# New step, piece and tile tables in the written order of an attention and FFN kernel

## The reference

```python
x = x + attention(layernorm(x))          # 16 heads of 16 features, causal
x = x + ffn(layernorm(x))
# attention: num = exp(rot(q) . rot(k) / 4), den = sum over ALL k of exp(q . k / 4), no rotation
#            y = where(causal, num / den, 0) @ v;   then y @ Wout + bout
# ffn: square(relu(x @ Ws1)) @ Ws2, and eight routed experts whose weight
#      trunc(softmax(top 2 logits)) is 0 except where one of the two weights is 1
```

## Time and profile before

| | us |
|---|---|
| median of 3 runs | 1680.91 |
| the profiled execution | 1680.97 |
| its span, first to last instruction | 1679.4 |
| ACT busy | 1586.1 (94%) |
| PE busy | 1487.9 (89%) |
| DVE busy | 848.6 (51%) |
| POOL busy | 526.9 (31%) |
| mean granted PE clock | 0.978 |

### The profile page before, as it was taken

One profiled execution on the slowest core, in us unless ns is written; L12 is line 12 of the kernel. 1 busy time (PEld: TensorE's weight loads), 2 busy tenths in 40 slices (PEclk: granted clock), 3 DMA queues, 4 the chain that ended last, 5 costly groups with the idle time before them and its releaser, 6 DMA issues.

```text
span 1679.4 us, 25467 instructions
## 1 busy us (share of the span) xinstructions
PE 1487.9 (89%) x8224; PEld 574.9 (34%) x8224; DVE 848.6 (51%) x1946; ACT 1586.1 (94%) x2639; POOL 526.9 (31%) x865
## 2 busy tenths in 40 slices
PE   2888989999999989999899999999999998999885
PEld 1322323333333333333343333333333333333323
DVE  5433434665346653566456553466535664455315
ACT  1899999999999999999999999999999999999990
POOL 3323233332233322333332322343223433333210
PEclk8998999999999999999999999999999999999997
DMA  5332332332434313333233234333143432332300
GB/s 160 97 120 91 94 114 91 124 94 76 129 104 138 111 38 123 122 121 104 89 116 123 95 91 130 114 116 104 51 129 114 129 114 65 115 123 82 95 26 26
DMA packets 95005, 172.05 MB, mean 102 GB/s; under 512 B 15504, under 2 KB 82064, under 8 KB 82576
## 3 DMA queue, kind: packets, MB, share of 16 engines
q1 hardware_dynamic: 94272, 169.15, 32.6%
q10 hardware_dynamic: 592, 1.18, 0.3%
HBM read 111.55 MB, written 58.72 MB: 101 GB/s over the span
## 4 chain that ended last, share of the span: by engine, by line
ACT 86%; PE 7%; issue 4%; DVE 2%; DMA 1%; SPq 0%; DVEq 0%; POOL 0%; ACTq 0%
ACT scores L488 56%; ACT probs L498 27%; ACT probs L500 3%; PE scores L544 2%; PE y_ps L573 1%; PE side L583 1%; PE scores L551 1%; PE side L602 0%; SPq L322 0%; DMA x_in<-in_L_attn_x 0%; PE scores L652 0%; DMA qk_parts<-parts 0%; PE scores L592 0%; PE scores L602 0%; DVEq L789 0%
## 5 line engine op out<-in xcount | busy, mean ns | idle before, releaser
L488 ACT ACTIVATE scores<-scores 128x1024 f32<-128x1024 f32 x1024 | 1067.1, 1119 | 24.5 <-PE scores L544 24.2
L544 PE MATMUL scores<-stack 96*128 96x512 bf16 x2048 | 584.6, 385 | 84.9 <-ACT scores L488 38.3
L498 ACT ACTIVATE probs<-scores 128x1024 f32<-128x1024 f32 x512 | 491.3, 1106 | 7.1 <-PE scores L551 5.7
L551 PE MATMUL scores<-stack 96*128 96x512 bf16 (+3 forms) x1536 | 337.3, 331 | 50.9 <-ACT scores L488 38.9
L394 POOL TENSOR_SCALAR_AFFINE_SELECT probs<-probs 128x256 f32<-128x256 f32 (+1 forms) x640 | 243.4, 408 | 392.4 <-ACT probs L498 224.5
L573 PE MATMUL y_ps<-probs,v_sb 128*32 128x512 f32 (+3 forms) x3072 | 331.8, 504 | 4.1 <-POOL probs L394 4.1
L544 PEld LDWEIGHTS scores<-stack 96*128 96x128 bf16 x2048 | 152.8, 97 | 493.8 <-ACT scores L488 203.5
L488 ACT ACTIVATION_READ_ACCUMULATOR scores<-scores 128x1 f32 x1024 | 297.3, 290 | 0.0
L404 POOL TENSOR_TENSOR parts<-rest,parts 128x512 bf16<-128x512 f32 x124 | 143.2, 1155 | 292.1 <-DVE parts L856 292.1
L551 PEld LDWEIGHTS scores<-stack 96*128 96x128 bf16 x1536 | 117.2, 98 | 307.9 <-ACT scores L488 158.0
L402 POOL TENSOR_TENSOR rot<-raw,cos_sb 128x512 f32<-128x512 f32 x62 | 89.0, 1436 | 397.2 <-DVEq L866 397.2
(11 more groups left out here) (121 smaller groups left out, 1062.7 us busy)
## 6 DMA issues: line engine op xcount, KB each, us to landing
stack<-qk_parts SPq DMA_DIRECT2D x762, 128.0 KB, 2.6
qk_parts<-parts SPq DMA_DIRECT2D x127, 384.0 KB, 2.6
out<-x_mid SPq DMA_DIRECT2D x32, 256.0 KB, 2.8
x_in<-in_L_attn_x SPq DMA_DIRECT2D x7, 1024.0 KB, 5.3
x_in<-in_L_attn_x SPq DMA_DIRECT2D x2, 512.0 KB, 4.5
stack<-qk_parts ACTq DMA_DIRECT2D x6, 128.0 KB, 4.4
probs<-in_L_attn_Wqkv SPq DMA_DIRECT2D x1, 512.0 KB, 5.8
cos_sb<-in_cos SPq DMA_DIRECT2D x1, 512.0 KB, 6.5
```

The lines of the kernel that those rows point to most:

```text
L488: nc.scalar.activation(src, src, ACT.Exp, scale=SCALE, accum_out=den[:, g % 2, i, j:j + 1]).then_inc(exp_done, 1)
L498: nc.scalar.activation(probs[:, chunk % 2, j, :], src, ACT.Exp, scale=SCALE).then_inc(exp_done, 1)
L544: mm = nc.tensor.matmul(tile[:, half * HALF:(half + 1) * HALF], q[:, j, i * P:(i + 1) * P], k[:, j, half * HALF:(half + 1) * HALF], start= ...
L551: mm = nc.tensor.matmul(tile[:, col:col + n], k[:, h, i * P:(i + 1) * P], q[:, h, q0:q0 + n], start=True, stop=True)
```

## The change

Only tables of numbers change: the order of the 50 steps, the step of each PV piece and of each side tile, and the single points. No instruction is added, removed or resized. Instructions move on all engines.

```diff
-ORDER = [5, (0,), 4, (1,), 3, (2,), 7, (3,), 6, (4,), 7]
+ORDER = [6, (0,), 1, (1,), 7, (2,), 5, (3,), 5, (4,), 8]
 PV_STEPS = [
-    (15, 17, 25, 27, 33, 35, 37, 40, 42, 43, 45, 48),
+    (13, 19, 23, 29, 30, 31, 36, 38, 42, 45, 47, 48),
...
-TAKE_Y = [47, 42, 37, 42]
+TAKE_Y = [43, 43, 36, 48]
-RECIPROCALS = (32, 25, 16, 25)
+RECIPROCALS = (22, 25, 20, 31)
 SIDE = [
...
-    {0: ("qk", 0), 5: ("ffn", 1), 7: ("route", 2), 8: ("turn", 1), 13: ("qk", 2), 17: ("ffn", 2),
-     22: ("norm", 0), 23: ("turn", 3), 26: ("ffn", 3), 29: ("norm", 1), 32: ("acc", 0), 36: ("acc", 1),
-     39: ("acc", 2), 46: ("xt", 0), 48: ("xt", 1)},
+    {0: ("qk", 0), 3: ("ffn", 0), 7: ("route", 2), 8: ("turn", 1), 10: ("qk", 2), 14: ("ffn", 1), 16: ("ffn", 2),
+     18: ("turn", 3), 23: ("norm", 0), 24: ("norm", 1), 27: ("acc", 0), 30: ("acc", 1), 33: ("acc", 2),
+     38: ("acc", 3), 42: ("ffn", 3), 49: ("xt", 0)},
...
-STATS2 = (1, 29)
-STATS1 = {(1, 49): 0, (2, 4): 1, (2, 11): 2, (2, 15): 3, (2, 45): 4}
-COPY = (1, 43)
-GAP = (1, 49)
-BRANCH = (3, 42)
+STATS2 = (1, 23)
+STATS1 = {(2, 0): 0, (2, 9): 1, (2, 12): 2, (2, 16): 3, (2, 48): 4}
+COPY = (1, 37)
+GAP = (2, 4)
+BRANCH = (3, 35)
```

More of the change, by code:

```diff
@@ L91 @@
 Y_FIRST, Y_LAST = [(0, 0), (3, 0)], [(3, 1), (4, 1)]
-TAKE_Y = [47, 42, 37, 42]
+TAKE_Y = [43, 43, 36, 48]
 LOW_LAG = 3
-RECIPROCALS = (32, 25, 16, 25)
+RECIPROCALS = (22, 25, 20, 31)
 SIDE = [
-    {0: ("v", 0), 4: ("qk", 0), 8: ("v", 1), 12: ("v", 2), 14: ("turn", 1), 20: ("qk", 2), 28: ("turn", 3),
-     30: ("v", 3), 35: ("norm", 0), 38: ("norm", 1)},
-    {0: ("qk", 0), 3: ("acc", 0), 5: ("turn", 1), 7: ("qk", 2), 15: ("acc", 1), 17: ("acc", 2),
-     21: ("turn", 3), 22: ("acc", 3), 30: ("t2", 0), 33: ("t2", 1), 34: ("t2", 2), 38: ("t2", 3),
-     40: ("route", 0), 44: ("ffn", 0), 47: ("route", 1)},
-    {0: ("qk", 0), 5: ("ffn", 1), 7: ("route", 2), 8: ("turn", 1), 13: ("qk", 2), 17: ("ffn", 2),
-     22: ("norm", 0), 23: ("turn", 3), 26: ("ffn", 3), 29: ("norm", 1), 32: ("acc", 0), 36: ("acc", 1),
-     39: ("acc", 2), 46: ("xt", 0), 48: ("xt", 1)},
-    {0: ("acc", 3), 1: ("xt", 2), 6: ("xt", 3), 8: ("qk", 0), 12: ("ffn", 4), 14: ("turn", 1), 20: ("ffn", 5),
-     23: ("qk", 2), 28: ("turn", 3), 35: ("ffn", 6), 38: ("ffn", 7)},
+    {0: ("qk", 0), 4: ("v", 0), 8: ("turn", 1), 10: ("v", 1), 15: ("qk", 2), 20: ("v", 2), 26: ("v", 3),
+     35: ("turn", 3), 40: ("norm", 0), 46: ("norm", 1)},
+    {0: ("qk", 0), 4: ("acc", 0), 6: ("turn", 1), 8: ("qk", 2), 12: ("acc", 1), 15: ("acc", 2), 18: ("turn", 3),
+     22: ("acc", 3), 30: ("t2", 0), 32: ("t2", 1), 34: ("t2", 2), 38: ("t2", 3), 39: ("route", 0),
+     41: ("route", 1)},
+    {0: ("qk", 0), 3: ("ffn", 0), 7: ("route", 2), 8: ("turn", 1), 10: ("qk", 2), 14: ("ffn", 1), 16: ("ffn", 2),
+     18: ("turn", 3), 23: ("norm", 0), 24: ("norm", 1), 27: ("acc", 0), 30: ("acc", 1), 33: ("acc", 2),
+     38: ("acc", 3), 42: ("ffn", 3), 49: ("xt", 0)},
+    {0: ("xt", 1), 2: ("xt", 2), 4: ("xt", 3), 6: ("qk", 0), 10: ("ffn", 4), 13: ("turn", 1), 15: ("ffn", 5),
+     24: ("qk", 2), 30: ("ffn", 6), 32: ("turn", 3), 39: ("ffn", 7)},
 ]
```

## The result

The changed kernel takes 1724.11 us (median of 4 runs, 1722.38 to 1730.55) against 1680.94 on the same chip (4 runs, 1680.88 to 1683.34): **slower by a ratio of 1.0261, 95% interval 1.0232 to 1.0288**. The direction was forecast, 1706 us was not: the time lies above the range of 1690 to 1721. The profiled run took 1729.71 us, span 1728.1, mean granted TensorE clock 0.960 for 0.978. The runs of the changed kernel spread over 8 us. One run of experiment 4, at 2293.4 us with a granted clock of 0.578, is in a slower state and is left out of the figures there.

A forecast was written before the change was run, and what follows sets the result against it. ACT was taken as the bound, losing time wherever PE's scores came late. On 1680.97, 14.7 + 9.1 + 3.5 + 2.1 - 3.8 - 3.5 + 2.7 = +24.8 gave 1706 us, range 1690 to 1721.

The forecast's parts named there:

- the 2.1: Third group's norm 0 and 1 on following steps, first PV piece closer behind chunk 0: 0.3 x 7 = 2.1 us lost.
- the prediction's own sign: Wrong if DVE's L972 for ffn 1 came before 15 us into the group, or ACT lost pace somewhere unnamed.
- the room: At each step PE may be late by 0.7 up to 1.1 us; ACT loses whatever exceeds this for good.
- Second group, 9.1: acc 2 behind step 15 waits until DVE has added acc 1: 1.3 x 7 = 9.1 us lost (6 to 11).
- Third group, 14.7: ffn 2 behind step 16 waits for DVE to empty ffn 1's bank: 2.1 x 7 = 14.7 us lost (7 to 21).
- The clock, +2.7: Lower PE clock behind the branch in five batches of seven instead of two: 2.7 us lost (-1.8 to 12).
- rival 3: Half clock behind the branch in all seven batches and in the third group's projection, 7 more: 1715 us, chance 0.24.
- The branch, 3.5: Fourth group: less ACT time covers the branch, a PV piece right behind: 0.5 x 7 = 3.5 us lost (0 to 6).
- First group, -3.8: Start of each first group, v 0 and last PV pieces now apart: 2 x 0.27 x 7 = 3.8 us gained.
- First batch, -3.5: Sixth den step fills a wait, qk half gone, chunk 2 waits no longer: 3.5 us gained (1 to 5).
- Rival 2: Only one of the second and third groups' waits counts, half of both terms: 1694 us, chance 0.14.
- Rivals 1 and 4: Rival 1: DVE in time, faster, 1673.7 us, chance 0.06. Rival 4: waits trade one for one, 1681, chance 0.04.

The follow-up runs named there:

- experiment 4: Changed kernel with ffn 1 of the third group at step 5, second group's acc 1 and 2 at 15 and 17, norm 1 at 26: 1715.69 us, ratio 1.0204.
- experiment 2: Changed kernel with acc 1 and acc 2 of the second group at steps 15 and 17 instead of 12 and 15: 1713.39 us, ratio 1.0171.
- experiment 1: Changed kernel with ffn 1 of the third group at step 5 instead of 14: 1735.90 us, ratio 1.0313.
- experiment 7: Kernel before with ffn 1 of the third group at step 15, behind qk 2, instead of 5: 1712.67 us, ratio 1.0179.
- experiment 5: Changed kernel with the scores of steps 4 to 9 of each third group multiplied twice: 1723.22 us, ratio 1.0236.
- experiment 11: Kernel before with qk 0 and v 0 of the first group trading steps 0 and 4: 1684.18 us, ratio 0.9999.
- experiment 3: Changed kernel with norm 1 of the third group at step 26 instead of 24: 1729.16 us, ratio 1.0276.
- experiment 8: Changed kernel with the third group's first statistics pair between qk 0's split and ffn 0: 1726.75 us, ratio 1.0261.
- experiment 9: Changed kernel with the edits of experiments 1 and 2, third group's turn 3 behind norm 0, norm 1 and acc tiles spread: 1720.53 us, ratio 1.0218.
- experiment 10: Kernel of experiment 9 with the third group's PV piece (2, 0) at step 31 instead of 28: 1698.63 us, ratio 1.0093.
- experiment 12: Kernel before with qk 0 first, and scores doubled behind the branch and in eleven steps of the first batch's second group: 1678.95 us, ratio 0.9979.

## Why the forecast was right in direction and wrong in size

- **Where the 24 us between 24.8 and 48.8 are.** The third group lost 13.9 more than its terms (14.7 and the 2.1), the two gains came out 10.5 worse, the second group 1.9 and the end 1.6 worse, and the fourth group 3.9 better. By the prediction's own sign it was wrong: ACT lost its pace at places that it hadn't named, steps 10 to 12 of the third group, 12 of the second, and 28 and 30 of the fourth.
- **What bounds it, and the room.** Right. ACT stays the bound, its loss explains the span to 0.1 us, and nothing was caught up again.
- **Second group, 9.1.** Right in place and cause (`acc` 2 behind L922), 11.0 measured. The 0.3 a batch too little are small roundings along the chain: L922 ended at 15.5, taken as 15.3, from there ACT's start took 1.6, taken as 1.5, and 1.4 was written down as 1.3. `acc` 1's own wait wasn't foreseen, but isn't a further cost. Shown by experiment 2.
- **Third group, 14.7: this is the step that failed, as a size; it measured 30.7.** The chain is the forecast one, confirmed from both sides by experiments 1 and 7. Three things made 32 out of 15. (a) The chain is 0.95 longer: I took the ffn tile, routing and turn from the earlier trace rows, where the tile stood apart from POOL's work; moved right behind the split, its square ran into POOL's part. With what else steps 10 to 17 lose, the queue's part there is 26.2 - 7 x 0.95 = 19.5, or 2.8 a batch (experiment 5). (b) The norm took 7 x 0.95 = 6.7, not a share of 2.1. I had looked at norm 0 and 1 standing close to each other, and not at what DVE has in front of norm 0: turn 3, which was moved to step 18, right ahead of it. (c) The lower clock, 5.7, all of it in the four batches with 6.8 us of it.
- **The sum of ends.** The range of this term, 7 to 21, was built for the chain alone. The norm's bound of 0.6 a batch (4 in all) was below the 0.95 measured, and once the first wait is gone these two steps lose 3.5 (experiment 1).
- **The clock, +2.7, put behind the branch.** The place was wrong. Behind the branch the clock fell in three full batches where it had fallen in two, not in five, and cost 0.5 to 0.7 in each, less than the 0.9 taken. It fell in the third group's bare steps, the second place of rival 3, which was priced at 7 and measured 5.7. The rule cited from the Trainium skill, TensorE: Matmul & The Clock Gate, would have had both places in every batch: the trace has it in six of seven at one and in three of seven at the other, so it agrees in direction and not in every batch.
- **The branch, 3.5.** Too much. The 1.94 that I took as fixed came from one batch and was the longest of seven; the branch cost nothing now. That its group still lost 2.3 is luck for the sum: 3.4 of its loss stands at steps 28 and 30, which I hadn't priced.
- **First group, -3.8.** Did not come: -0.5. Step 0 lost 0.21 and now loses 0.11, step 1 still loses 0.26. I had put the 0.27 on `v` 0 and the last pieces together; experiment 11 shows that the tile's kind changes nothing. What holds PE at step 1 stays open.
- **First batch, -3.5.** Came out at +3.7. The sixth den step filled its 1.03, but the first num step came 0.57 later than the 51.97 that I took as fixed, and steps 10 and 11 lost 1.6, about what step 5 no longer did, so the first group gained 0.2 only. The other three groups lost 4.0 more, and I had given them no term. The batch now spends 34.0 us at the lower clock for 27.6. How much of the 4.0 is the change stays open: in the traces of experiments 1 to 5 and 8 to 10, whose first batch has the same work but for small shifts, its loss was anything from 9.1 to 15.3 us, and in those on the kernel before (7, 11 and 12) 10.2 to 13.1. The start of the first exponential varies as well, 39.1 to 39.9 in five of the fourteen profiled executions and 41.1 to 42.0 in the others. Both lie in the spread of the runs.
- **The rivals.** Rival 2 (one wait only) is half right, in a way that I had not written: waits do cover for one another, not those of the second and third group, which add up, but those within the third. Rivals 1 and 4 are out, and rival 3 was right on the third group's clock only. No rival had the second wait at norm 0.

## What to carry over

Where tiles share one in-order queue, a moved tile is to be priced with everything that stands ahead of it there after the move, and so is the next tile behind it: curing the first wait in such a chain uncovers the second (here `ffn` 2, then norm 0, then the PV piece at step 28), and only the three cures together were worth most of it. A duration taken from one batch is one sample (1.94 of 1.09 to 1.94), and it holds only with its neighbours on the other engines: a two-input DVE operation that comes to stand beside POOL's work is another operation. And behind every stretch in which PE is left with little work, look at the granted clock.
